# A maximum over partitions, one early operand split and 96 small stores, each issued at another place of a two-layer cross-attention kernel

## What is computed

```
x = x + tanh(g_xattn[0]) * L0_xattn(layernorm(x), ctx)   # 32 heads, 8 key heads, dim 128, RMS norm on q and k
x = x + tanh(g_ffn[0])   * L0_ffn(layernorm(x))          # clip(x*xs) @ clip(w*ws) / (xs*ws)
x = x + tanh(g_xattn[1]) * L1_xattn(layernorm(x), ctx)   # 16 heads, 4 key heads, dim 96
x = x + tanh(g_ffn[1])   * L1_ffn(layernorm(x))          # 8 routed rank-16 adapters
```

## Time and profile before

| | |
|---|---|
| median of 3 runs (lowest to highest) | 2687.97 us (2687.37 to 2689.05) |
| profiled execution, its own time | 2688.13 us |
| span in its trace, first to last instruction | 2686.3 us |
| PE busy | 2626.0 us, 98% |
| DVE busy | 1549.8 us, 58% |
| ACT busy | 1286.6 us, 48% |
| POOL busy | 969.9 us, 36% |
| granted clock of PE, mean | 0.994 of full speed |

### The profile page before, as it was taken

The page is one execution under the profiler, slowest core; times in us unless marked ns, Lnnn a source line. Parts: engine busy times, 40 slices in busy tenths (PEclk is TensorE's granted clock), DMA queues, the critical chain, the costliest instruction groups (busy, mean ns, idle before and its releaser), DMA issues. The chain is left out here.

```text
span 2686.3 us, 38860 instructions
## 1 busy us (share of the span) xinstructions
PE 2626.0 (98%) x13508; PEld 2240.2 (83%) x13508; DVE 1549.8 (58%) x2750; ACT 1286.6 (48%) x2846; POOL 969.9 (36%) x842
## 2 busy tenths in 40 slices
PE   8999999999999999999999999999999999999998
PEld 6788778888888888877888888888898999788887
DVE  7767786565676333346566656655445311777766
ACT  6655664323434333356555555555252322755544
POOL 2555423354232111137555555555300000544430
PEclk9999999999999999999999999999999999999999
DMA  4566565565554233336333333333230232433311
GB/s 170 191 210 201 166 228 201 165 207 174 197 170 161 83 102 98 108 95 198 105 108 105 107 102 110 104 100 95 103 109 1 76 100 74 122 94 81 88 44 56
DMA packets 339050, 336.40 MB, mean 125 GB/s; under 512 B 127233, under 2 KB 275449, under 8 KB 338857
## 3 DMA queue, kind: packets, MB, share of 16 engines
q1 hardware_dynamic: 337768, 331.82, 39.6%
q10 hardware_dynamic: 1088, 2.10, 0.2%
HBM read 237.35 MB, written 96.49 MB: 124 GB/s over the span
## 5 line engine op out<-in xcount | busy, mean ns | idle before, releaser
L45 PE MATMUL pb<-p_ws,p_xs 128*128 128x512 f32 (+1 forms) x1124 | 437.9, 390 | 23.2 <-DVE p_c L1266 10.7
L47 PE MATMUL pb<-p_ws,p_xs 128*128 128x512 f32 (+1 forms) x1124 | 428.4, 381 | 0.0
L46 PE MATMUL pb<-p_ws,p_xs 128*128 128x512 f32 (+1 forms) x1124 | 427.7, 381 | 0.0
L847 POOL TENSOR_TENSOR p_xr<-p_xf 128x512 f32<-128x512 f32 x175 | 238.3, 1374 | 440.6 <-PE pb L47 199.0
L1762 ACT ACTIVATE at_p<-pb,at_nmax 112x487 f32<-112x487 f32 x256 | 171.3, 670 | 318.9 <-DVE at_nmax L1843 318.9
L45 PEld LDWEIGHTS pb<-p_ws,p_xs 128*128 128x128 f32 x1124 | 213.5, 190 | 60.6 <-issue 18.3
L1266 DVE TENSOR_TENSOR p_c<-pb,p_c 128x512 f32<-128x512 f32 (+1 forms) x280 | 175.7, 659 | 149.8 <-PE pb L47 148.1
L1598 POOL TENSOR_TENSOR at_k<-at_kr,at_k 128x488 fp32r<-128x488 f32 (+1 forms) x94 | 116.4, 1238 | 369.8 <-DVE at_k L1857 369.8
L47 PEld LDWEIGHTS pb<-p_ws,p_xs 128*128 128x128 f32 x1124 | 213.2, 190 | 36.2
L46 PEld LDWEIGHTS pb<-p_ws,p_xs 128*128 128x128 f32 x1124 | 213.8, 190 | 32.5
L1862 DVE TENSOR_TENSOR at_ptlo<-pb,at_pthi 125x448 fp32r<-125x448 f32 (+1 forms) x256 | 148.0, 620 | 93.9 <-ACT at_pthi L1784 93.9
(11 more groups left out here) (268 smaller groups left out, 6407.1 us busy)
## 6 DMA issues: line engine op xcount, KB each, us to landing
p_xf<-xT_d SPq DMA_DIRECT2D x23, 1024.0 KB, 5.7
p_raw<-in_L_xattn_Wq_dram SPq DMA_DIRECT2D x32, 512.0 KB, 4.2
at_raw<-in_L_xattn_Wo_dram SPq DMA_DIRECT2D x64, 256.0 KB, 2.7
xT_d<-p_xf SPq DMA_DIRECT2D x15, 1024.0 KB, 5.2
qT_d<-p_qstage SPq DMA_DIRECT2D x56, 256.0 KB, 2.7
at_qr<-qT_d SPq DMA_DIRECT2D x64, 224.0 KB, 3.1
at_rb<-rT_d SPq DMA_DIRECT2D x64, 224.0 KB, 3.5
at_kr<-kT_d SPq DMA_DIRECT2D x64, 187.5 KB, 2.8
```

Source lines behind the costliest of these rows:

```text
L45: pe.matmul(out, stat_hi, mov_hi, start=start, stop=False)
L46: pe.matmul(out, stat_hi, mov_lo, start=False, stop=False)
L47: return pe.matmul(out, stat_lo, mov_hi, start=False, stop=stop)
L847: pool.tensor_tensor(xr[:, n % 10, 1, :, :], src[:, a[0], HK * a[1]:HK * a[1] + HK, :], src[:, b[0], HK * b[1]:HK * b[1] + HK, :], op).the ...
```

## The change

Three independent edits. POOL's all-reduce moves out of the list's event WX to Q's projection, behind the cut of slab 15 (the last odd slab that is cut while column 0 is on PE); DVE's reduction to `most` stays at WX, and the five small instructions that follow the all-reduce move behind `norm_q(12)`. In layer 1 alone, DVE cuts k's high part of unit 1 ahead of the four row maxima of unit 0 rather than behind them. And the store of each unit's row sums is issued by ACT, right behind its own copy, rather than by SP; this holds for all 96 units of both layers.

```diff
@@ POOL, first_layer @@
-                        elif e[0] == "WX":
-                            pool.wait_ge(wf_most, 1)
-                            pool.partition_all_reduce(most[:], most[:], P, bass.bass_isa.ReduceOp.max).then_inc(wf_reduced, 1)
                         elif e[0] == "WQ" and e[1] % 2:
                             cut(e[1])
                     for s in range(KS + 1, NQ * KS, 2):
                         cut(s)
+                        if s == 2 * KS - 1:
+                            pool.wait_ge(wf_most, 1)
+                            pool.partition_all_reduce(most[:], most[:], P, bass.bass_isa.ReduceOp.max).then_inc(wf_reduced, 1)
@@ DVE, first_layer @@
-                    def w_scale():
+                    def w_most():
                         dve.wait_ge(wf_topped, KS)
                         dve.tensor_reduce(most[:], w_tops[:], AX.X, ALU.max).then_inc(wf_most, 1)
+
+                    def w_scale():
                         dve.wait_ge(wf_reduced, 1)
...
                         elif e[0] == "WX":
-                            w_scale()
+                            w_most()
...
                         norm_q(n)
+                        if n == 2 * TT - 2:
+                            w_scale()
@@ SP, attend @@
-                def spread_sums(u):
-
-                    sp.wait_ge(r_copied, u + 1)
-                    sp.dma_start(rT_d[u], rt[:, u % 2, :]).then_inc(r_stored[u % 2], 16)
-
...
                 for u in range(U):
-                    if not flip and u <= NB:
-                        spread_sums(u)
                     if u + 3 < U:
                         load_qk(u + 3)
                     if u + 2 < U:
                         load_v(u + 2)
-                    if not (not flip and u <= NB):
-                        spread_sums(u)
@@ ACT, attend @@
+                def spread_sums(u):
+                    act.wait_ge(r_copied, u + 1)
+                    act.dma_start(rT_d[u], rt[:, u % 2, :]).then_inc(r_stored[u % 2], 16)
+
...
                     copy_sums(u)
+                    spread_sums(u)
                     if u + 2 < U:
                         cut_q(u + 2)
@@ DVE, attend @@
                 yield
+                if flip:
+                    cut_k(1)
                 for h in range(G):
                     neg_max(0, h)
                     yield
-                cut_k(1)
+                if not flip:
+                    cut_k(1)
```

## The result

| | before | after |
|---|---|---|
| median of 5 runs each (lowest to highest) | 2688.76 us (2687.37 to 2690.12) | **2674.30 us** (2672.25 to 2676.28) |
| profiled execution, its own time | 2688.13 us | 2673.95 us |
| span | 2686.3 us | 2672.2 us |
| PE busy | 2626.0 us | 2618.0 us, 98% |
| ACT busy | 1286.6 us | 1295.0 us, 48% |

The ratio of the runs is 0.995, 95% interval 0.9939 to 0.9962: 10.2 to 16.4 us less. The forecast was 11.5 less; the spans of the two profiled executions differ by 14.1.

The account below looks back on a forecast made before the run. PE, nearly always busy, was taken as the bound, with time to win only where it waits or runs at lower clock. From 2688.13 us, -8.7 - 5.3 + 2.5 = -11.5 gave 2676.6 us; range 2673.5 to 2683.

Parts of the forecast that it names:

- (e): Whole kernel: everything goes as forecast, 2676.6 us; chance 0.64.
- Part 1: Pass w = 2: moving the all-reduce removes PE's stop near 800 and the lower clock behind it, -8.7 us.
- 1.60 of clock: Behind PE's stop near 800: ten matmuls took 3.34 us where 1.74 was due at 2.4 GHz.
- Rival (b): POOL's x sum at 800.51 was really released by PE, so moving the all-reduce gives nothing: 2685.3 us; chance 0.05.
- two cases: Q's projection: all-reduce with its silence ends at 896.2, or at 904 if an equal configuration change precedes it; no cost.
- Part 2: Layer 1's start: cutting unit 1's k earlier removes PE's 3.49 us wait and brings unit 2's first exponential forward, -5.3 us.
- 0.4 allowed for loads: Layer 1's start: 0.4 us taken off the 5.75 gain for Wo's first slab and unit 2's loads.
- Part 3: Attention: ACT's store of row sums lengthens units 2 to 7 of layer 0, covered elsewhere, +2.5 us.
- d: ACT's added time per unit for its copy wait and store issue: about 0.42 us, bounds 0.10 and 0.66.
- Rival (a): ACT's store is free, since layer 0's ring also waits for DVE's maximum: 2674.1 us; chance 0.12.
- rival (d): ACT's store issue is held up by SP's burst of loads, near 3.3 us per unit: 2716.7 us; chance 0.04.
- PE's waits for the inverted sums or the cut of q grow by 0.4 each: Layer 0, units 2 to 7: expected sign as these units take 8.4 us rather than 8.0.

Follow-up runs that it names:

- `reduce_only`: Kernel before with only the all-reduce moved behind slab 15 in Q's projection: 2677.93 us, ratio 0.9961 to before.
- `store_only`: Kernel before with only the row-sum store issued by ACT behind its copy instead of by SP: 2691.60 us, ratio 1.0012 to before.
- `reduce_four`: Changed kernel with SP issuing the row-sum store again and four all-reduces, behind slabs 15, 17, 19 and 21: 2685.33 us, ratio 0.9990 to before.
- `reduce_idle`: Kernel before with the all-reduce moved to Q's projection and one of a constant tile, waiting for nobody, in the old place: 2685.37 us, ratio 0.9987.
- `reduce_next`: Kernel before with the all-reduce three x sums later and DVE's use of its result in Q's projection: 2676.64 us, ratio 0.9957 to before.
- `store_later`: Changed kernel with ACT's row-sum store one place later, behind the cut of q(u + 2): 2673.07 us, ratio 0.9945 to before.
- `store_twice`: Changed kernel with a second store of the same row sums, issued by ACT directly behind the first: 2679.46 us, ratio 0.9969 to before.
- `reduce_twice`: Changed kernel with SP issuing the row-sum store again and a second all-reduce directly behind the first: 2671.17 us, ratio 0.9940 to before.

## Why the prediction was right

The time was 2674.3 for 2676.6 forecast, and inside the range, 0.8 above its low end; the case was (e), with every part of the forecast sign. The mechanisms of parts 1 and 2 held. The size of part 1 was too small, and the forecast of part 3 came out by two small errors that cancel.

**Part 1** (forecast -8.7, bounds -6.5 to -8.9): the gap of 7.30 and the 1.60 of clock both came back whole, 8.91 in the profiled pair (A 63.11 to 54.20). The 0.2 I kept for a short wait left over was wrong; PE has no new wait for p_c between 780 and 860. This term was undersized, for a second reason too: I took one execution's stop for the kernel's. Its size in three executions is 8.9, 9.2 and 10.8, and the median of `reduce_only` is 9.5 below before's, the ratio 10.5. My upper bound of 8.9 was thus no bound; what I had as 1.60 for the clock was about 2.9 in `store_only` (10.78 less the gap of 7.93 between matmuls). Rival (b), the sum released by PE, is refuted. That the 8.5 us belong to a change of program, which I took from the earlier trace rows, is shown by the two calls in a row. The stretch ahead of the call, hidden in the earlier trace rows, is 5.75 us long now. The Trainium skill ("GPSIMD Engine Reference", section on instruction dispatch) says that the first call to a freshly loaded program pays about 6 us with no visible instruction; the traces agree, with 5.66 to 6.03. They show a second stretch on the way back, of 6.7 to 9.1.

For what POOL pays in Q's projection I had two cases, ready for slab 17 at 896.2 or at 904. It was between them: 890.9, in a stretch that comes 9.8 us earlier than before, so 900.7 on the forecast's scale. As ACT's high part of slab 17 was ready at 887.7 (886.54 and 1.14 for two slabs), the slab is 3.2 us late, and this costs nothing. The cover stands up: in `reduce_four` PE's only stop is in product 14, where I had put the first read of these slabs, and it took the fourth change of program to cause it.

**Part 2** (forecast -5.3): C is 13.66 against 18.80 to 18.98 in the four variants without it (`reduce_only`, `store_only`, `reduce_idle`, `reduce_next`), -5.1 to -5.3. In before's own profiled execution C was 19.28; unit 1's last exponential starts 15.6 us after unit 0's first there, and 15.2 to 15.3 in the others. So the profiled pair shows -5.6. The chain that I used, unit 0's last exponential plus 7.59, holds to 0.14 us (2279.20 + 7.59 = 2286.79, measured 2286.93); so little of the 0.4 allowed for loads was needed, though PE waits 0.31 for Wo's slab.

**Part 3** (forecast +2.5): 8.39 for 8.00 in six units is +2.3, and 0.2 more in unit 0 (7.66 for 7.46); layer 1 is covered, its units stay at 7.59. That the sum is +2.5 is luck: d was 0.39 and not 0.42, and unit 0 made up for it. I took the 0.25 of issue as a price that ACT pays wherever it issues. `store_later` shows that it is hidden beside a running instruction, and only a wait that empties the engine lays it open. Rival (a), a free store, is wrong for this kernel and right for one with the store one place later.

I had also said that unit 0 is covered; it costs the 0.2, and what rival (d) describes is seen there. ACT's issue and SP's issue of k beside it in unit 0:

```profile
1179.41 0.52 ACTq L1762 DMA_DIRECT2D rT_d<-at_rt  x1
```
```profile
1179.38 0.61 SPq L1523 DMA_DIRECT2D at_kr<-kT_d  x1
```

ACT's issue begins 0.03 us after SP's and takes 0.52 instead of 0.25. So d is 0.66 in this unit, 0.2 above the cover of 0.46. It is the only one of the 96 that takes over 0.3 us, and unit 0's is so in `store_only`, `store_later` and `store_twice` too; in `store_later` it costs nothing, as unit 0 stays at 7.46 there. In unit 2 SP's issue of v took 1.59 us around ACT's, and ACT's stayed at 0.25. Who holds up whom is thus not the same each time; that the two issues share something was not tested by a run of its own.

The step "PE's waits for the inverted sums or the cut of q grow by 0.4 each" failed: they stayed. The unit grew inside PE's busy time.

**The rest.** Of the 14.1 us between the profiled spans, the edits make 8.9 + 5.6 - 2.5 = 12.0. 0.8 were there before the first edit (the x sum at 779.59 against 780.39). Some 0.4 lie between the two attentions. That stretch, from layer 0's last copy of row sums to layer 1's first exponential, took 386.19 us before and 385.77 in the changed kernel, and 384.5 to 387.5 in the thirteen profiled executions. With SP's store five of nine are near 384.6 and four near 386; with ACT's store all four are at 385.8 or above. Whether part 3 has a share in that is open; a single execution can differ by 1.6 us there without it. Another 0.8 came in the last 60 us, where PE in the kernel before ran below its full clock,

```profile
2668.00:2672.00 4.00, 3.30 (x26) 0.89 0.35 131
2672.00:2676.00 4.00, 4.00 (x21) 0.68 0.02 4
```

and in the changed one did not. In the profiled executions of this study the clock fell in this stretch in all five kernels without part 2, and in two of the eight with it (`store_twice`, `reduce_twice`). Whether that is chance or an effect of part 2 on what comes 300 us later, no run tells; it stays open.

## What to carry to other kernels

This all-reduce on POOL costs some 13 us where its own row shows 0.38: a stretch ahead of it and one behind it, once per change of program and not per call. Put such calls together, and where POOL would wait anyway. When ScalarE must issue a DMA of its own result, put one independent instruction between the two: the wait is then over when the issue comes up, and the issue hides beside that instruction. And measure a stop in more than one execution before bounding what its removal brings.

## What the runs showed of the hardware

- POOL's change of program: 5.66 to 6.03 us ahead of the all-reduce, with no instruction in the trace but two configuration instructions of 1 to 13 ns at its start; 6.7 to 9.1 us behind it; 0.48 from one call to the next directly behind it. What sets the spread on the way back is open: it was 8.5 to 9.1 where the call came behind a wait for DVE, 6.7 to 7.6 elsewhere.
- ScalarE's queue issues a DMA beside a running activation: 0.25 us at no cost, and 0.52 at no cost in unit 0 of `store_later`. Behind a wait for its own result the same issue costs 0.39 us with the wait, and a second one behind it 0.35. An issue that began some 0.03 us after one of SP took 0.52 instead of 0.25, in four kernels.
- A stop of PE of 3.95 us was followed by more time at 1.2 GHz than one of 7.13 (slower pace of the matmuls for 6.1 us in `reduce_idle`, 3.5 before; granted 0.58 over 805 to 810 there): shortening a stop need not shorten what it costs behind it.
